# Two of five transposed-weight copies move from ScalarE to VectorE in the last batch

## The reference

```python
# x: (4, 128, 32, 32) f32; gn = group norm with 32 groups
x = x + mixing(gn(x), W, b)              # y = relu(cos-similarity of pixels)^2 applied to W x + b
g = gn(x)
offset = conv3x3(conv3x3(g, w1, b1), w2, b2)          # 72 channels: 4 groups x 9 taps x (y, x)
val = bilinear samples of g at (pixel + tap + offset), 4 groups, 9 taps
x = x + relu(einsum('ogck,bgckhw->bohw', wd, val))    # deformable convolution, 128 -> 128
```

## Time and profile before

| | |
|---|---|
| runs (3) | 515.77 us median, 515.76 to 515.89 |
| profiled execution | 515.51 us, of which the span from first to last instruction is 513.8 us |
| mean granted TensorE clock | 0.947 |
| TensorE busy | 428.8 us, 83% of the span |
| VectorE busy | 344.2 us, 67% |
| ScalarE busy | 224.7 us, 44% |
| GpSimd busy | 140.7 us, 27% |

### The profile page before, as it was taken

The page is one execution under the profiler, slowest core; times in us unless marked ns, Lnnn a source line. Parts: engine busy times, 40 slices in busy tenths (PEclk is TensorE's granted clock), DMA queues, the critical chain, the costliest instruction groups (busy, mean ns, idle before and its releaser), DMA issues.

```text
span 513.8 us, 9711 instructions
## 1 busy us (share of the span) xinstructions
PE 428.8 (83%) x3881; PEld 304.9 (59%) x3881; DVE 344.2 (67%) x582; ACT 224.7 (44%) x404; POOL 140.7 (27%) x179
## 2 busy tenths in 40 slices
PE   2899799967998988779998987878798976888886
PEld 2666465734665656557665654657565654666665
DVE  4619996499988983954657992745979538199400
ACT  2046133224565453414655453314765333178640
POOL 3266441343872102102763101101210101031100
PEclk9999799997999989989999989879998987999999
DMA  3400000201111113011101112011210121023211
GB/s 122 169 1 1 1 1 1 46 1 21 22 22 22 22 22 65 6 40 31 33 15 27 22 22 56 23 33 41 43 24 20 25 64 33 20 52 64 42 33 33
DMA packets 22187, 17.23 MB, mean 34 GB/s; under 512 B 1981, under 2 KB 20669, under 8 KB 22141
## 3 DMA queue, kind: packets, MB, share of 16 engines
q1 hardware_dynamic: 21884, 16.07, 12.9%
q10 hardware_dynamic: 256, 0.52, 0.7%
HBM read 3.74 MB, written 3.28 MB: 14 GB/s over the span
## 4 chain that ended last, share of the span: by engine, by line
PE 58%; DVE 24%; ACT 7%; issue 5%; DMA 3%; ACTq 2%; SPq 1%; DVEq 0%
PE psB L719 13%; PE psB L506 12%; PE psA L586 8%; DVE wpix L1342 6%; PE psV L695 5%; PE psA L506 5%; PE psT L672 5%; ACT wcell L897 3%; DVE tent L1323 2%; PE psT L662 2%; DMA hwin<-hwin 2%; PE psA L562 2%; DVE tent L1317 2%; DVE combo L1135 2%; ACT val L910 2%
## 5 line engine op out<-in xcount | busy, mean ns | idle before, releaser
L897 ACT ACTIVATE wcell<-psT 128x512 f32<-128x512 f32 (+1 forms) x160 | 83.4, 552 | 82.3 <-PE psT L672 73.6
L1342 DVE TENSOR_TENSOR wpix<-tent 128x512 f32<-128x512 f32 (+1 forms) x160 | 107.1, 720 | 16.0 <-PE psT L672 15.0
L672 PE MATMUL psT<-ident,wpix 128*128 128x128 f32 x576 | 86.5, 283 | 14.5 <-ACT wcell L897 13.5
L672 PEld LDWEIGHTS psT<-ident,wpix 128*128 128x128 f32 x576 | 66.9, 144 | 38.8 <-issue 28.7
L447 POOL COPY strips<-hring 128x256 f32<-128x256 f32 x64 | 43.3, 702 | 155.8 <-PE psT L662 155.8
L424 POOL TENSOR_TENSOR sim<-rel 128x512 f32<-128x512 f32 x48 | 60.3, 1276 | 62.4 <-ACT rel L858 62.4
L719 PE MATMUL psB<-val,wd_sb 128*128 128x256 f32 x288 | 73.5, 412 | 3.6 <-issue 3.6
L719 PEld LDWEIGHTS psB<-val,wd_sb 128*128 128x128 f32 x288 | 57.7, 206 | 15.6 <-issue 7.2
L695 PE MATMUL psV<-wcell,hwin 64*32 64x144 f32 x2048 | 48.5, 300 | 13.3 <-DMA hwin<-hwin 13.3
L910 ACT ACTIVATE val<-psV 128x576 f32<-128x576 f32 x64 | 44.0, 688 | 34.2 <-PE psV L695 22.7
L506 PE MATMUL psB<-g_p 128*128 128x512 f32 x144 | 44.6, 448 | 6.7 <-DVE g_p L1075 6.7
(11 more groups left out here) (166 smaller groups left out, 498.0 us busy)
## 6 DMA issues: line engine op xcount, KB each, us to landing
hwin<-hwin SPq DMA_DIRECT2D x64, 128.0 KB, 2.5
out<-yout SPq DMA_DIRECT2D x16, 128.0 KB, 1.8
x_all<-x SPq DMA_DIRECT2D x1, 1536.0 KB, 8.9
off_scr<-sim SPq DMA_DIRECT2D x4, 288.0 KB
combo<-sim SPq DMA_DIRECT2D x20, 32.0 KB
val<-w SPq DMA_DIRECT2D x1, 576.0 KB
wd_sb<-wd SPq DMA_DIRECT2D x1, 576.0 KB
x_all<-x SPq DMA_DIRECT2D x1, 512.0 KB, 3.5
```

Source lines behind the costliest of these rows:

```text
L672: last = pe.transpose(bank[:, at:at + P], wpix[:, t % 2, k, 2 * h:2 * h + 2, :].rearrange("p g q -> p (g q)"), ident[:, :])
L897: act.activation(wcell[:, t % 2, taps[0]:taps[-1] + 1, :, :].rearrange("q k h p -> q (k h p)"), bank[:, 0:len(taps) * G // 2 * P], ACT.Cop ...
L1342: dve.tensor_tensor(w, ty, tx, ALU.mult).then_inc(s["weights_done"], 1)
```

## The change

In the last batch VectorE takes the groups with index 1 and 3 of `TURNS`, "taps 1" and "taps 2", out of PSUM, and counts them in a semaphore of its own, `turn_taken`. ScalarE keeps "taps 0", "windows 0", "taps 3" and "taps 4". TensorE's waits ask the semaphore of whichever engine takes the group (`taken`), and the first half of a tile's sampling waits for VectorE's last copy as well. In VectorE's list a copy stands ahead of a product of the same slot. The slots of the products in the last batch come from `W_LAST`, which puts the five products of tile t at slots 1, 2, 4, 6 and 7 of tile t-2.

```diff
+        W_LAST = {t: tuple(K * (t - 2) + slot for slot in (1, 2, 4, 6, 7)) for t in range(2, ROWT)}
         W_AT = {2: (0, 1, 3, 5, 6), 3: (9, 10, 12, 14, 15), 4: (18, 19, 21, 23, 24),
                 5: (31, 32, 33, 35, 36), 6: (37, 38, 40, 44, 45), 7: (47, 48, 50, 51, 52)}
...
-        def freed(n, idx):
-
-            return TAKES * n + idx + 1 + FREE0
+        DVE_TAKES = (1, 3)
+
+        def by_dve(b, idx):
+
+            return b == B - 1 and idx in DVE_TAKES
+
+        def taken(b, t, idx):
+
+            if t < 0:
+                b, t = b - 1, t + ROWT
+            if by_dve(b, idx):
+                return s["turn_taken"], len(DVE_TAKES) * t + DVE_TAKES.index(idx) + 1
+            done = TAKES * (ROWT * b + t) + idx + 1 + FREE0
+            if b == B - 1:
+                done -= len(DVE_TAKES) * t + sum(i < idx for i in DVE_TAKES)
+            return s["turn_free"], done
...
                 back = (t, idx - 2) if idx >= 2 else (t - 1, idx - 2 + TGROUPS)
-                pe.wait_ge(s["turn_free"], freed(ROWT * b + back[0], back[1]))
+                pe.wait_ge(*taken(b, *back))
...
-                    pe.wait_ge(s["turn_free"], freed(ROWT * b + t, TGROUPS - 1))
+                    pe.wait_ge(*taken(b, t, TGROUPS - 1))
+                    if b == B - 1:
+                        pe.wait_ge(*taken(b, t, DVE_TAKES[-1]))
                     pe.wait_ge(s["crossed_odd" if t % 2 else "crossed_even"], 32 * (ROWT // 2 * b + t // 2 + 1))
...
-                    act.wait_ge(s["turn_free"], freed(ROWT * b + t, idx))
+                    act.wait_ge(*taken(b, t, idx))
...
-                        if k in TURN_SLOT:
+                        if k in TURN_SLOT and not by_dve(b, TURNS.index(TURN_SLOT[k])):
                             evacuate(b, t, TURN_SLOT[k])
...
+            def take_turned(b, t, what):
+
+                idx, i = TURNS.index(what), int(what.split()[1])
+                dve.wait_ge(s["sampled"], VGROUPS * (ROWT * b + t - 1) + SAMPLED0)
+                dve.wait_ge(s["turned"], TGROUPS * (ROWT * b + t) + idx + 1 + TURNED0)
+                taps = TAPS[i]
+                dve.tensor_copy(wcell[:, t % 2, taps[0]:taps[-1] + 1, :, :].rearrange("q k h p -> q (k h p)"),
+                                psT[:, (TGROUPS * t + idx) % 2, 0:len(taps) * G // 2 * P]).then_inc(s["turn_taken"], 1)
...
-                        for tile, slots in W_AT.items():
+                        if k in TURN_SLOT and by_dve(b, TURNS.index(TURN_SLOT[k])):
+                            take_turned(b, t, TURN_SLOT[k])
+                        for tile, slots in (W_AT if nxt is not None else W_LAST).items():
```

More of the change, by code:

```diff
@@ L229, in mix_deform_kernel @@
             "g_sample g_acc g_conv g_relu g_out g_stored "
-            "swap_ready own_ready crossed_even crossed_odd dist_done fold_done tent_done weights_done turned turn_free "
+            "swap_ready own_ready crossed_even crossed_odd dist_done fold_done tent_done weights_done turned turn_free turn_taken "
             "sampled val_free dconv_done orelu_done yout_done settled grid_ready out_first out_second").split()}
```

## The result

The changed kernel takes 529.23 us (median of 4 runs, 528.39 to 529.51) where the one before took 515.83 beside it (4 runs, 515.76 to 516.09). The ratio is 1.0256, 95% interval 1.0238 to 1.0274: 13.4 us slower, with 12.7 forecast. The profiled execution took 529.35 us, its span is 527.4 where it was 513.8.

A forecast was written before the change was run, and what follows sets the result against it. It took the ring of TensorE and ScalarE, 5.19 us a tile, to set the pace, with VectorE nearly full. 515.77 + 11.2 (tiles 0 to 6) + 1.5 (clock) = 528.5 us, range 523.8 to 533.0.

The forecast's parts named there:

- The ring: Last batch: TensorE and VectorE wait on each other through both copies, 7.03 us a tile instead of 5.19, +1.84.
- The copy's price: VectorE's copy out of PSUM: 0.605 us for its place in the queue, 0.68 until its signal.
- the lower end at 0.46: VectorE's copy as short as L1326's 0.46 us: +9.0 without the clock, 524.8 us.
- The tiles: Last batch: +2.05 us in tile 0, 1.84 in each of tiles 1 to 5, together +11.2 without the clock.
- The clock: TensorE's stalls in six tiles lower its granted clock: 0.25 us a tile, 1.5 in all.
- the second rival: TensorE's clock is low for most of the ring: +11.2 and 6 to 8.6, 533 to 536 us; chance 0.12.
- That is all an idle ScalarE could give: some 0.23 us a tile: ScalarE's queue delays taps 2 by 0.12 us, the next taps 0 about as much; under 2 us in eight tiles.
- faster: ScalarE's queue limits and VectorE has room: 1.8 us less, 514.0 us; chance 0.03.
- throughput only: Copies close no ring, only VectorE's serial work counts: about +8.2 us, less at tile 6, 524.0; chance 0.11.

The follow-up runs named there:

- load_only: Kernel before with the new product slots plus two extra VectorE copies a tile (tiles 0-5) that nobody waits for: 514.42 us, ratio 0.9996, stage 0.0.
- tents_ahead: Changed kernel with each tile's three tent operations moved behind the last product of the tile before: 520.57 us, stage +6.28 against the kernel before.
- four_banks_after: Changed kernel with turned groups going round four PSUM banks instead of two in the last batch: 520.13 us, stage +4.50 against the kernel before.
- keep_warm: Changed kernel with three filler matmuls in TensorE's stall ahead of taps 4, tiles 0 to 5: 527.72 us, stage 51.62 where the changed kernel has 52.59.
- light_after: Changed kernel without the three tent operations for tiles 2 to 7 of the last batch: 515.13 us, ratio 1.0007 to the kernel before, stage +0.64.

## Why the prediction was right

**The ring, right.** Forecast 7.03 a tile, measured 7.06 to 7.07. Its terms: copies 0.69 long and 0.60 to the next start (0.68, 0.605), tents 2.23 (2.28), TensorE's part to the next first copy 2.34 (2.26), VectorE's idle time 0.80 (0.7). That it is a ring, and not the load, is shown by three runs that keep all the work: load_only (0.0), tents_ahead (+6.28) and four_banks_after (+4.50). The two terms that were off nearly cancel, 0.05 too much for the tents and 0.08 too little for TensorE's part. And the ring is not the only way to lose: without it the queue alone, with TensorE waiting behind it, still costs the 6.28 or 4.50.

**The copy's price, right**, from L1148; the lower end at 0.46 did not come. The Trainium skill, "Advanced Engine Details and Errata", section VectorE Performance Modes, gives an f32 copy a doubled rate only with both ends in SBUF, and this trace agrees: the copy out of PSUM takes 0.69 for 512 columns, where L1342, with one source and both ends in SBUF, takes 0.46 to 0.54 for 576.

**The tiles, right in form.** +11.2 was forecast without the clock. Measured are 13.19 for the stage less 1.4 for the clock, 11.8. The missing 0.6 are 0.28 in tile 0, where the forecast overlooked that the next taps 1 waits for ScalarE's copy of taps 4 (6.58 and not 6.3); 0.03 to 0.04 in each of the next five tiles; and 0.11 in tile 6, where taps 2 to taps 4 takes 1.60 (495.62 to 497.22), not 1.49. The end behind tile 7 stayed, 25.2 against 25.1, as forecast.

**The clock, right in size, less so in kind.** 1.5 was taken, 1.4 is what keep_warm and the distances give. That the size is so close is luck: it was thought of as 0.25 in each of six tiles; it is 0.4 and 1.1 in two and nothing in four. It fell 1.1 and 0.7 us after TensorE came back (455.65 to 456.7, 469.66 to 470.4), not 1.8, so more of the ring's part was slow each time. The Trainium skill, "TensorE: Matmul & The Clock Gate", section on HAM oscillation, tells of a kernel whose clock falls in each wait; here six stalls, five of them of 2.2 to 2.5 us, brought two falls, so this kernel did the same only in part, and the second rival did not come.

**Step that failed: "That is all an idle ScalarE could give: some 0.23 us a tile".** It is 0.05 at most. The bound compared ScalarE's start with 0.64 us behind the first transpose, and called the 0.12 and 0.11 that were over a queue. Idle engines take such a group after 0.73 (ScalarE, tile 0) to 0.77 (VectorE, light_after), so of the 0.76 and 0.75 (469.16 to 469.91) at taps 2 and taps 0 at most 0.03 and 0.02 are queue. The rival "faster" rested on the 0.23. The same 0.1 us is missing in two terms of the forecast itself: from the transposes of taps 0 and 1 to VectorE's copy it is 1.20 (492.91 to 494.11) and not 1.09 + 0.03, and in tile 6 the 0.64 + 0.03 is 0.77.

**The rival "throughput only"** is not what happened: VectorE idles 0.80 us in every tile of the changed kernel, so the length of its queue is not the limit. Where it is the limit, in tents_ahead, the loss is 6.28 and not 8.2.

**Not settled.** What decides in which stall the clock falls was not tried, nor why the first group of eight tap transposes is picked up about 0.1 us later than the windows. That GpSimd's strip copies lengthen the tents (L1339 0.83 beside them, 0.76 away from them) is read from timelines alone; no run moved just these copies.

## What to carry to other kernels

Before moving a copy to another engine, ask not whether that engine has time, but what stands in its queue between this copy and the next one that the same partner waits for: that stretch is added to the partner's ring, here 3.44 us of tents and products that had been free. Load without a waiter can be hidden by a lead, a waiter behind a full queue cannot. The cheapest remedy is the order of the queue: moving the tents out from between the copies gave back 6.9 of the 13.2 us. And where a ring of turn, copy, turn sets the pace with both its engines at some 83 to 85% busy, count the buffers first: two more PSUM banks gave 6.7 us where moving the copies lost 13.4.

## What the runs showed of the hardware that I had not expected

- An engine starts on the first four of eight tap transposes 0.73 to 0.77 us after they begin, VectorE (0.77, light_after) and ScalarE (0.73 idle, 0.76 busy) alike, while four transposes take 0.63. So about 0.1 us of that wait is pick-up and no queue. For the windows, four transposes by themselves, it is only 0.67 (465.46 to 466.13 in the kernel before).
- With much the same stall in every tile the granted clock fell behind two of six and not behind the other four.
- VectorE's operations on SBUF differ in length with their place relative to GpSimd's copies: tents 2.23 to 2.28 us a tile beside them, 1.97 to 2.07 (mostly) away from them. That the one causes the other was not tested.
